# Projections of the first half of the rows placed between the two halves of the transposes, in a decoder block on one core

## What is computed

```python
x = x + self_attention(layernorm(x))            # ... ends in einsum('bnf,cf->bnc', out, w_out)
# cross-attention, q = layernorm(x), k = v = ctx
qh = (q @ Wq.T + bq) / sqrt(16)                 # 256 -> 256
scores = einsum('bhqd,bhkd->bhqk', qh, kh); attn = softmax(scores)
x = x + (einsum('bhqk,bhkd->bhqd', attn, vh) @ Wo.T + bo)
# latent attention on rmsnorm(layernorm(x)) * norm1
q = x_n @ Wq.T                                  # 256 -> 256, then rope
latent = layernorm(x_n @ Wdkv.T)                # 256 -> 128
k, v = latent @ Wuk.T, latent @ Wuv.T           # k then rope
# causal softmax attention, Wo; then the experts
```

## Time and profile before

| | |
|---|---|
| three runs, us | 2644.41, 2649.71, 2651.07 |
| median, us | 2649.71 |
| the profiled execution's own time, us | 2647.83 |
| its span, first to last instruction, us | 2646.1 |
| mean granted TensorE clock | 0.981 |
| PE busy | 2502.5 us, 95% |
| DVE busy | 1386.6 us, 52% |
| ACT busy | 1065.0 us, 40% |
| POOL busy | 318.4 us, 12% |

### The profile page before, as it was taken

How to read it: one execution, slowest core, us unless ns; L and a number is a source line. 1 busy time by engine, 2 the same in 40 slices (tenths; PEclk the granted TensorE clock), 3 DMA queues, 4 the chain that set the end, 5 groups by cost and what they waited for, 6 DMA issues and landing times.

```text
span 2646.1 us, 44027 instructions
## 1 busy us (share of the span) xinstructions
PE 2502.5 (95%) x16830; PEld 1673.4 (63%) x16831; DVE 1386.6 (52%) x3834; ACT 1065.0 (40%) x2284; POOL 318.4 (12%) x436
## 2 busy tenths in 40 slices
PE   6999999999999999999999999999999899959998
PEld 4555666665555665665555665565556566649997
DVE  3344368854333377853333577834333578744443
ACT  3444134554444134644444235534443226612221
POOL 2000010210010110210000111200100011231111
PEclk9999999999999999999999999999999999979999
DMA  3000000000000000000000000000000000051111
GB/s 107 13 13 0 17 1 1 2 15 20 24 25 1 17 1 2 2 14 30 21 19 1 17 1 2 2 20 24 25 15 1 17 1 2 2 196 53 54 54 38
DMA packets 33491, 57.30 MB, mean 22 GB/s; under 512 B 7916, under 2 KB 24505, under 8 KB 32921
## 3 DMA queue, kind: packets, MB, share of 16 engines
q1 hardware_dynamic: 28552, 41.73, 5.0%
q0 software_dynamic: 4752, 13.02, 1.3%
HBM read 40.41 MB, written 14.32 MB: 21 GB/s over the span
## 4 chain that ended last, share of the span: by engine, by line
PE 91%; ACT 3%; DVE 3%; issue 1%; POOL 1%; DMA 0%; SPq 0%; DVEq 0%; POOLq 0%
PE ps L1235 11%; PE ps L975 10%; PE ps L947 9%; PE ps L920 9%; PE ps L1265 6%; PE ps L905 6%; PE ps L965 5%; PE ps L1340 5%; PE ps L1354 5%; PE ps L930 4%; PE ps L1200 4%; PE ps L860 3%; PE ps L876 2%; PE ps L1100 1%; PE ps L1084 1%
## 5 line engine op out<-in xcount | busy, mean ns | idle before, releaser
L1442 DVE TENSOR_REDUCE neg_max<-ps 128x1 f32<-128x128 f32 (+7 forms) x256 | 193.7, 758 | 562.8 <-PE ps L950 549.4
L813 ACT ACTIVATE arena<-ps 128x512 f32<-128x512 f32 (+1 forms) x640 | 320.1, 552 | 276.0 <-PE ps L1235 273.2
L1235 PE MATMUL ps<-arena 32*128 32x256 f32 (+1 forms) x2560 | 386.9, 379 | 0.0
L1235 PEld LDWEIGHTS ps<-arena 32*128 32x128 f32 x2560 | 272.9, 184 | 111.8 <-issue 72.2
L1200 PE MATMUL ps<-arena 32*128 32x512 f32 (+3 forms) x1536 | 334.7, 527 | 3.9 <-ACT arena L803 3.9
L975 PE MATMUL ps<-arena 128*128 128x512 f32 (+3 forms) x768 | 319.7, 503 | 4.9 <-ACT arena L744 0.8
L744 ACT ACTIVATE arena<-ps 128x512 f32<-128x512 f32 (+3 forms) x384 | 188.2, 491 | 292.0 <-PE ps L965 286.2
L947 PE MATMUL ps<-arena 128*128 128x512 f32 (+3 forms) x768 | 289.8, 487 | 7.1 <-ACT arena L755 7.1
L920 PE MATMUL ps<-turned_t,arena 128*128 128x512 f32 x512 | 232.6, 604 | 1.1 <-ACT turned_t L715 1.1
L947 PEld LDWEIGHTS ps<-arena 128*128 128x128 f32 x768 | 140.3, 190 | 140.7 <-issue 122.8
L755 ACT ACTIVATE arena<-ps,neg_max 128x128 f32<-128x128 f32 (+7 forms) x256 | 189.0, 738 | 54.3 <-DVE neg_max L1442 54.0
(11 more groups left out here) (220 smaller groups left out, 3539.8 us busy)
## 6 DMA issues: line engine op xcount, KB each, us to landing
arena<-in_w_qkv SPq DMA_DIRECT2D x32, 384.0 KB
arena<-in_w SPq DMA_DIRECT2D x2, 4096.0 KB, 16.7
xin<-in_x SPq DMA_DIRECT2D x5, 1024.0 KB, 5.5
xres_ids<-sorted_res SPq DMA_DIRECT2D x35, 129.0 KB, 2.3
xin<-sorted_rows SPq DMA_DIRECT2D x35, 128.0 KB
w_out<-in_w_out SPq DMA_DIRECT2D x1, 1024.0 KB
out<-xin,out_row POOLq DMA_INDIRECT x35, 2.9
sorted_res<-xin SPq DMA_DIRECT2D x4, 129.0 KB
```

What stands on the lines that cost most here:

```text
L813: nc.scalar.activation(mprobs_t[n % BUFS][:, j, 0:QUARTER + more], ps[:, item_bank(n, j), 0:QUARTER + more], ACT.Exp).then_inc(mexp_done, 1)
L1235: return nc.tensor.matmul(ps[:, item_bank(n, j), kb * QUARTER:kb * QUARTER + n_q], k_heads_t[rows_j, g, keys_at:keys_at + P], q_heads_t[ro ...
L1442: nc.vector.tensor_reduce(neg_max[:, par, t:t + 1], ps[:, buf:buf + 2, :].rearrange("p a n -> p (a n)")[:, 0:n], AX.X, ALU.max, negate=Tru ...
```

## The change

Only TensorE's and VectorE's programs change. No product, transpose or copy of the computation is added or taken away.

- In the last head, the wait for both copies of the head before is split: TensorE waits for the copy of bank 6 at the start and for that of bank 7 before part 3, where bank 7 is first written.
- The first half of the cross turn is done inside the projection, before its last row tile (`between`). No `keep_warm` stands before the second half. The queries of the first half stand before the second half's transposes. The queries go to banks 4 to 7, where the turned rows were, so that `cross_scores(0)`, in banks 0 to 3, can stand between the two halves' queries; it now also waits for all adds of the projection. VectorE takes the second half's queries after it has taken the first tile's scores.
- The latent turn's second half stands after the latents and the queries of the first half. One product of `keep_warm` is left of five. The latents of the first half now wait for all adds of the cross projection, since they use its banks.

```diff
-            WAITS = {TURN_CROSS: 3, TURN_LATENT: 5, TURN_GATE: 1}
+            WAITS = {TURN_CROSS: 0, TURN_LATENT: 1, TURN_GATE: 1}
...
-                def project(use, lhs, rhs, bias=None, turn_use=None):
+                def project(use, lhs, rhs, bias=None, turn_use=None, between=None):
 
                     for t in range(NT):
+                        if between is not None and t == NT - 1:
+                            between()
...
-                pe.wait_ge(out_taken, b * (2 * HEADS) + h * 2)
+                pe.wait_ge(out_taken, b * (2 * HEADS) + h * 2 - 1)
...
                 for t in range(NT):
+                    if t == 3:
+                        pe.wait_ge(out_taken, b * (2 * HEADS) + h * 2)
                     products(h, h % 2, t)
...
+                project(PROJ_SELF, [attn_t[:, k, :] for k in range(HEADS)], [w_out[:, k, :] for k in range(HEADS)],
+                        between=lambda: turn_half(b, TURN_CROSS, rows, 0))
+
+                def cross_queries(n, m):
+
+                    for kt in range(KT):
+                        last = nc.tensor.matmul(ps[:, 4 + KT * n + m, :], xw_q[:, kt, m * P:(m + 1) * P],
...
                     if t == 0:
-                        pe.wait_ge(xq_taken, b * 4 + 4)
+                        pe.wait_ge(proj_added, b * (PROJS * NT) + (PROJ_SELF + 1) * NT)
+                        pe.wait_ge(xq_taken, b * 4 + 2)
                         pe.wait_ge(xk_made, b * 2 + 2)
...
+                    if t == 4:
+                        pe.wait_ge(xq_taken, b * 4 + 4)
...
+                turned(TURN_CROSS, 0)
+                for m in range(KT):
+                    cross_queries(0, m)
+                turn_half(b, TURN_CROSS, rows, 1)
                 cross_scores(0)
+                turned(TURN_CROSS, 1)
+                for m in range(KT):
+                    cross_queries(1, m)
...
+                turn_half(b, TURN_LATENT, rows, 0)
+                pe.wait_ge(proj_added, b * (PROJS * NT) + (PROJ_CROSS + 1) * NT)
+                turned(TURN_LATENT, 0)
+                latents(0)
+                latent_queries(0)
+                latent_queries(1)
+                turn_half(b, TURN_LATENT, rows, 1)
+                turned(TURN_LATENT, 1)
+                latents(1)
+                latent_queries(2)
+                latent_queries(3)
...
+                take_queries(0)
                 for t in range(NT):
...
+                    if t == 0:
+                        take_queries(1)
```

More of the change, by code:

```diff
@@ L1047, in _ @@
                 pe.wait_ge(xkv_taken, b * 3 + 3)
-                project(PROJ_SELF, [attn_t[:, k, :] for k in range(HEADS)], [w_out[:, k, :] for k in range(HEADS)])
-                turn(TURN_CROSS)
-                for n in range(2):
-                    turned(TURN_CROSS, n)
-                    for m in range(KT):
-                        i = KT * n + m
-                        for kt in range(KT):
-                            last = nc.tensor.matmul(ps[:, i, :], xw_q[:, kt, m * P:(m + 1) * P],
-                                                    turned_t[:, kt, n * BANK:(n + 1) * BANK],
-                                                    start=(kt == 0), stop=(kt == KT - 1))
-                        last.then_inc(xq_done, 1)
+                project(PROJ_SELF, [attn_t[:, k, :] for k in range(HEADS)], [w_out[:, k, :] for k in range(HEADS)],
[3 more added lines that the diff above has]
+                        last = nc.tensor.matmul(ps[:, 4 + KT * n + m, :], xw_q[:, kt, m * P:(m + 1) * P],
+                                                turned_t[:, kt, n * BANK:(n + 1) * BANK],
+                                                start=(kt == 0), stop=(kt == KT - 1))
+                    last.then_inc(xq_done, 1)
                 def cross_scores(t):
                     if t == 0:
-                        pe.wait_ge(xq_taken, b * 4 + 4)
+                        pe.wait_ge(proj_added, b * (PROJS * NT) + (PROJ_SELF + 1) * NT)
+                        pe.wait_ge(xq_taken, b * 4 + 2)
                         pe.wait_ge(xk_made, b * 2 + 2)
@@ L1082, in cross_values @@
                         pe.wait_ge(xpv_taken, b * (2 * NG) + use - 1)
+                    else:
+                        pe.wait_ge(xq_taken, b * 4 + 4)
                     for h in range(GROUP):
@@ L1121, in _, with latents @@
                         TURN_CROSS_OUT)
-                turn(TURN_LATENT)
-                for n in range(2):
-                    turned(TURN_LATENT, n)
+                def latents(n):
                     for t in range(4 * n, 4 * n + 4):
@@ L1131, in _, with latent_queries @@
                     last.then_inc(mlat_done, 1)
-                for i in range(NT // 2):
+                def latent_queries(i):
                     for t in range(2 * i, 2 * i + 2):
@@ L1520, in _, with take_queries @@
                                lambda h: normed_rows(b, NORM_CROSS, h, xres, rows, scale, rows_ready))
-                for i in range(4):
-                    n, m = divmod(i, KT)
-                    dve.wait_ge(xq_done, b * 4 + i + 1)
-                    nc.vector.tensor_scalar(xq_t[:, m, n * BANK:(n + 1) * BANK], ps[:, i, :], bq[:, m:m + 1],
-                                            float(XHD) ** -0.5, ALU.add, ALU.mult).then_inc(xq_taken, 1)
+                def take_queries(n):
+                    for m in range(KT):
+                        i = KT * n + m
+                        dve.wait_ge(xq_done, b * 4 + i + 1)
+                        nc.vector.tensor_scalar(xq_t[:, m, n * BANK:(n + 1) * BANK], ps[:, 4 + i, :], bq[:, m:m + 1],
+                                                float(XHD) ** -0.5, ALU.add, ALU.mult).then_inc(xq_taken, 1)
                 def cross_out(c, j):
```

## The result

| | before | changed |
|---|---|---|
| median of the runs compared, us | 2650.38 (4 runs, 2644.41 to 2651.07) | 2613.18 (4 runs, 2612.24 to 2617.61) |
| the profiled execution's own time, us | 2647.83 | 2612.24 |
| its span, us | 2646.1 | 2610.5 |
| mean granted clock | 0.981 | 0.985 |

The account below looks back on a forecast made before the run. TensorE's own work was taken to bound the kernel (91% of the chain that ended last). Gains of 14.4 and 25.9 less 3.2 make 37.1 us, from median 2649.7 to 2612; forecast 2603 to 2620, range 2602 to 2629.

Parts of the forecast that it names:

- Part 1: Last head, split wait: context products start 3.6 us earlier per batch, 14.4 in all; lower bound 1.8 per batch.
- Part 2: Cross turn: second scores 5.5 us earlier per batch, plus 3.9 in all up to the fourth scores; 25.9 together.
- GpSimd's add beside VectorE: Cross turn: line 618's add, 4.17 us, lies beside VectorE's takes and first scores; taken to cost nothing.
- The bound of 2.9: Cross turn: cost if VectorE were held until GpSimd's add ends, under 2.9 us a batch.
- Part 3: Latent turn: later latents for VectorE put TensorE 0.8 us later per batch, -3.2 in all.
- Its bound of 1.6: Latent turn: 1.6 us lost if all of VectorE's lateness goes through.
- The clock at the new waits: Rival: clock falls at new waits in cross or latent turn, some 9 us in all, 2621; chance 0.12.
- The other rivals: Cross turn only idle products: 2628, 0.05; split wait does nothing: 2627, 0.05; clock low through score loop: 2692, 0.02.

Follow-up runs that it names:

- warm_wait: Kernel before, wait in the last head unsplit, with three idle products of 128x512 put ahead of it; 2640.14 us against 2651.10, ratio 0.9962.
- after_again: The changed kernel once more, unchanged; 2617.03 us against 2651.30 for the kernel before, ratio 0.9869.
- after_later: The changed kernel with eight more small products at the start of the first batch's program; 2613.03 us against 2651.30 for the kernel before, ratio 0.9866.
- latent_order: Changed kernel, latent turn's second-half transposes between the first half's two query groups, no idle product; 2601.42 us against 2651.10 for the kernel before, ratio 0.9807.
- split_only: Kernel before with only the last head's wait split; 2628.30 us against 2651.87, ratio 0.9925.
- cross_only: Kernel before with only the cross turn's part of the change; 2630.55 us against 2651.87, ratio 0.9913.
- latent_only: Kernel before with only the latent turn's part of the change; 2658.71 us against 2651.87, ratio 1.0023.
- latent_chase: latent_order with GpSimd's memsets moved behind its scales and second-half transposes ahead of all queries; 2601.49 us against 2651.30 for the kernel before, ratio 0.9807.

## Why the prediction was right

By its own steps, in the first batch's times:

- **Part 1, 3.6 a batch: right.** The context products stand 3.62, 3.99, 3.80 and 3.69 us closer to the end of the head before, 15.1 together where 14.4 were forecast. The transposes, the ScalarE copy at 269.09, the product and the two transposes came in the order of the working, and the context products are at 270.65, of which 0.72 is the start's lead: 271.37 in before's time, against the 271.4 worked out. No releaser was named in the earlier trace rows, and taking it for the copy of bank 7 held. The split of the gain was a little off: warm_wait puts some 1.3 of it on the clock, not 1.8.
- **Part 2, 25.9: right, 26.1.** The first new wait is 0.93, forecast 1.15. The second scores stand 5.4 earlier, forecast 5.5 (331.69 - 321.97, less the 4.34 at the head). From the second to the fourth scores it takes 330.08 - 321.97 = 8.11, forecast 7.9, and 9.48 before, so this gave 1.4 in the first batch, forecast 1.5; together 6.8, measured 6.77. In the other batches it gave 1.0, 1.0 and 1.1, forecast 0.8. One step in it was wrong: the second pair of takes ends at 322.83 and VectorE's next maximum starts at 322.84, in time for the scores, so they delay nothing, and the third scores come 3.84 after the second. The 8.11 comes from the loop itself: in the first batch the fourth scores come 4.27 after the third before and after (336.90 to 341.17, and 325.81 to 330.08), and 3.9 in the other batches.
- **GpSimd's add beside VectorE costs nothing: right.** Line 618 runs from 316.33 to 320.49. Beside it VectorE's two takes take 1.41 and its maximum and subtraction 1.44 each, and the maximum without the add (322.84) takes 1.44 too. The bound of 2.9 wasn't needed.
- **Part 3, -0.8 a batch: the sign right, the size 1.07.** The working met each step to 0.1: latents at 376.04 + 11.1 = 387.1 and 395.6 (forecast 387.1 and 395.5), the rotations 401.7 (401.55). The rotated pair for the first query turn ended at 395.83, that is 406.9 (406.8), and TensorE went on 0.15 later; the last pairs ended at 409.6 (409.5), and TensorE's third block of turns, at 408.6 before, at 409.65. The step that failed is the last: 409.5 was compared with 409.1, TensorE's time when already late, and the semaphore's 0.1 behind each of VectorE's ends was left out. 4 x 0.27 = 1.1 us too little. Its bound of 1.6 held it. What the experiments add: four idle products fewer bought nothing, because VectorE's chain was what ended last there, and the same pieces in another order, without the last idle product, gain where this one loses.
- **The clock at the new waits (2621): fell in no batch,** nor in one of after_again or after_later. The stretch from the first half's queries to the first scores, transposes with waits of 0.8 and 0.9 around them, is at 1.00 (window 315 to 318 above), and so are the latents. Only latent_order fell once, behind a wait of 1.49. The rule of the Trainium skill (TensorE: Matmul & The Clock Gate, Part 4: PE-mode transpose) that was set against the change, that transposes don't count as work for the clock, would have had it fall there; the rows don't agree with it. That stretch is 2.3 us long and so a weak test, no longer than the shortest wait behind which before's clock fell (2.35). A longer one is in the same trace: 48 transposes and nothing else on TensorE for 5.4 us, at full clock.

```profile
360.60:366.00 5.40, 5.35 (x48) 5.11 (x48) 3.76 (x16) 1.00 (x3) 0.00 (x0) 1.00 0.02 3
```

The other rivals fell too: part 2 gave far more than its 2.6 of idle products, and part 1 did what it says.

- **The term that the sum left out** is the clock in stages that the change doesn't touch. In the profiled execution it was small: +0.7 at the start, -1.6 in the chunks of batch 3 and -0.4 from the gates on, so the sum of 36.9 in place and the 35.6 of the span differ by little. In the single parts, median against sum in place, it was large: 8.5 us for split_only, -4.7 for cross_only, -2.5 for latent_only. A range of 2602 to 2629 had room for it, but not by its own working. That the median met the forecast to 1 us is in part luck: parts 1 and 2 gave 0.7 and 0.2 more than forecast and part 3 took 1.0 more, and after_again, the same kernel, came out at 2617.0.

## What to carry to other kernels

Before you take idle products out or put work in their place, follow the engine that the next wait is for. In the cross turn the moved products and scores started VectorE's chain earlier, and the second scores came 5.4 us earlier by it; in the latent turn the same edit put eight query products ahead of the latents that VectorE was waiting for, and lost a microsecond. Feed the chain that ends last first, then fill behind it: latent_order and latent_chase do the same work as part 3 with one idle product less, and are 1.7 and 3.2 us a batch better (0.7 of the 3.2 came with the moved memsets). And measure an edit of a few microseconds by the lead at marks around its place, not by the total, as long as the clock in untouched stages moves the total by 5 us or more.

## What the runs showed of the hardware that I had not expected

- The granted clock fell to half in the middle of a stage in which TensorE was busy (12.24 of the 14 us before the fall at 2129.5), and stayed there for 10 us of work without a gap. The products of this stage have 32 rows on the partitions (32x512). The same work was at full clock in three of four batches.
- The same kernel fell in different batches in two executions (in batch 3; in batches 1 and 3). In before and its copy with eight more products the fall stood in batch 3 for 6.8 us and in batch 1 for 17.1.
- Behind one and the same wait of TensorE, 3.04 us, the clock stayed low for 3.4 us in some batches and for 6.8 in others, which moved the time to the next scores by up to 1.2 us.
- TensorE ran 48 transposes of 128x128 in a row for 5.4 us, and the granted clock stayed at 1.00.
- A copy of 128x8 on VectorE took 4.38 us beside GpSimd's memsets, 0.17 without them, while VectorE's reads of PSUM ran at their usual 1.44 beside GpSimd's add of 4.16 us.
